# Constants of attention made in the projection, six query and key transfers a head, diagonal sums from a second column of ones

## The chip, the cores and the metric

The kernel runs on one core of a Trainium2 chip. The core has five engines with queues of their own: TensorE (PE; matmuls, results in PSUM), VectorE (DVE), ScalarE (ACT), GpSimd (POOL) and SyncE (SP, which here only issues transfers). They run freely and meet at semaphores. Sixteen DMA engines move data between HBM and SBUF. The metric is the device time of one execution in microseconds.

## The reference

The program computes four blocks with residuals on x of shape (2, 2048, 256). The change is in the first one, attention:

```python
x = x + attn_a(layernorm(x), Wq, Wk, Wv, Wc, terrace_mix, index_decays, mega_decays)
x = x + ffn(layernorm(x), ...)       # 16 experts, top 2, and a shared one
x = x + attn_b(layernorm(x), ...)    # gated linear attention over routed memories
x = x + ffn(layernorm(x), ...)

# attn_a: 16 heads of 16, segments of 64 rows
scores  = q @ k.T / 4, causal
out_t   = softmax(scores where the key's segment is the row's or the one before) @ v
att     = softmax(scores)
pcs     = (att * exp(index_decays)).sum(rows of a segment)          # (segments, L)
mega    = clip(exp(mega_decays * 64), 0, 2)
w       = scan over segments: carry = carry * mega + pcs, outputs the carry before
w       = w / (w.sum(-1) + 1e-5)
kv      = einsum(w, k, v);  out_lin = q @ kv
tw      = sigmoid(terrace_mix)
y       = (tw * out_t + (1 - tw) * out_lin) @ Wc.T
```

## The kernel before

The phases follow each other with a barrier of all engines between: `phase_project`, `phase_attend`, `phase_merge`, `phase_moe` (experts), `phase_route`, `phase_gla`, `phase_final`, `phase_moe`. A phase is one block with a hand-written order of instructions for each engine; semaphores named in the code tie them. There is no scheduler: what stands in a queue runs in that order.

`phase_project` (lines 78 to 338) takes x in eight stretches of 512 rows: layer norm, transposes, the products q, k and v. Queries and keys are split into three bf16 parts (`part`, SyncE stores them at line 135 to `q_parts` and `k_parts`, each [3, 512, 2048] in DRAM), since a float32 score is made of six bf16 products. Values are stored with a 17th column of ones per tile of 128 rows (`vv`, `EV = 17`, memset at line 156), so that a product with them yields the sum of the weights too. SyncE's last issues are `v_tok` and `k_tok` (lines 141 and 143), and it waits for them before the phase ends.

`phase_attend` (348 to 907) goes over 32 heads (2 batches of 16). A head has 16 tiles of 128 query rows; four tiles make a group (`QUADS`), so there are 128 groups, numbered g. Per group:
- TensorE writes a window of scores (`window`, line 745: for each tile its own 128 keys and the 64 before, with a mask) and then 4 or 6 blocks of up to 1024 scores of earlier keys (`scores`, 764). All go to a ring of three PSUM buffers `S`, so a block waits for the exponential three places before it (`s_E`).
- VectorE takes row minima (scores are negated) of the window (`window_minima`, 655) and of each block (`minima`, 663), ScalarE the exponentials (`window_exps` into `Tt`, 579, and `exps` into `E` with row sums into `rs`, 591).
- TensorE transposes the window's probabilities (`transposes`, 777), VectorE copies them out (`keep_transposed`, 683), TensorE multiplies them with the values (`values`, 797; `vs` holds the values shifted by 64 rows for the tiles' first halves), VectorE scales the result into `Y` (`outputs`, 689).
- The row sum of the window without the 64 keys that are also in a block, needed to join window and blocks, is a VectorE reduction of `Tt` (`diag_sums`, 670). GpSimd forms the weights of the parts (`differences` 510, `weights` 516), between its steps VectorE inverts the total (`inverses`, 679), and TensorE adds the weighted probabilities up into `pcs` (`sums`, 818), one group later, between the blocks of the next one.
- Once a head, GpSimd makes the outer products of keys and values (`products`, 537, in three portions of 5, 5 and 6), and TensorE, ScalarE and VectorE turn `pcs`, multiply and normalise (841 to 864, 604 to 620, 702).

A group's order on VectorE, from line 718: window minima of the next group, its blocks' minima with the copy of the transposed behind the second and inverses and outputs behind the third, then `tops`, `normalise` in the fourth group, `diag_sums`. SyncE loads queries, keys and values of a head one head ahead into two buffers (`load_qk`, `load_kv`). `sq` and `sk` hold six slots of 16 rows, pairs of parts.

The constants are made in `phase_attend`'s preface: five small loads on SyncE ahead of the first head (425 to 427), the gate `tw`, `eid` and sixteen `decay` blocks of 32x32 on ScalarE (570 to 576), a mask on GpSimd (507), three copies to the other partitions behind the loads of two heads (455), for which TensorE waits ahead of the second group: `pe.wait_ge(spread, 48)` (869).

In `phase_moe` GpSimd scatters rows to their experts (line 1288), 64 transfers one after another, and clears a buffer of blank rows ahead of them (1276 to 1278) in the first of the two calls.

## Time and profile before

| | us |
|---|---|
| median of 3 runs | 2676.49 |
| lowest and highest | 2672.58, 2676.88 |
| the profiled execution | 2675.66 |
| its span, first to last instruction | 2674.0 |
| projection | 0 to 127 |
| attention | 127 to 1252 |

A page gives busy times of each engine, waits by what released them, and groups of instructions by line. A timeline row has start, duration, engine, line, operation, names of what is written and read, shapes and count, and in brackets the engine's idle time before it with what ended it. Names have the phase's letters in front: `pj_` projection, `at_` attention, `am_` kept from attention to the merge, `m_` experts. PEld is the loading of a matmul's stationary operand. Stretches are given as start and end in us of the span.

### The profile page before, as it was taken

To read this page: it belongs to the slowest core of one execution; us is meant where nothing else is said; L and a number is where in the kernel's file an instruction comes from. 1 tells how busy PE (TensorE), PEld (TensorE's weight loads), DVE (VectorE), ACT (ScalarE), POOL (GpSimd) and SP (SyncE) were. 2 spreads that over 40 slices of the span, in tenths; PEclk is the share of its full clock that TensorE was granted. 3 is DMA by queue.
4 is the path that set the end of the run, shared out by engine and by line. 5 is a ranking of instruction groups with operands and counts; after the bars stand their busy time and mean duration, and the time that the engine had idled before them with its cause. 6 is when DMAs were issued, how large, how long until landed. Compare 5 with 4: busy or idle time off the path is not lost. (4 is left out here: it accounts for less than half of the span.)

```text
span 2674.0 us, 72919 instructions
## 1 busy us (share of the span) xinstructions
PE 2301.8 (86%) x27120; PEld 1535.0 (57%) x27120; DVE 1920.6 (72%) x4760; ACT 1564.0 (58%) x3827; POOL 1237.5 (46%) x2277
## 2 busy tenths in 40 slices
PE   8689999999999999997987944499999999688791
PEld 5435454454544544444756834377777777565681
DVE  6578888888888888884664656277777776476465
ACT  5467777777777777774352322366666665465230
POOL 3324444444444444445674536545544444247461
PEclk9879999999999999998898965699999999689896
DMA  6711111111112111112436644301111111553555
GB/s 217 244 47 38 39 38 39 39 36 38 35 37 65 36 37 38 39 38 83 147 121 205 219 163 170 108 21 50 50 46 50 50 40 32 173 190 122 144 156 200
DMA packets 187403, 243.45 MB, mean 91 GB/s; under 512 B 41400, under 2 KB 144709, under 8 KB 185136
## 3 DMA queue, kind: packets, MB, share of 16 engines
q1 hardware_dynamic: 160656, 182.07, 22.1%
q0 software_dynamic: 19872, 50.41, 5.5%
q10 hardware_dynamic: 6528, 6.31, 0.8%
q8 instruction: 222, 3.64, 0.6%
q14 instruction: 125, 1.02, 0.1%
HBM read 136.09 MB, written 106.50 MB: 91 GB/s over the span
## 5 line engine op out<-in xcount | busy, mean ns | idle before, releaser
L668 DVE TENSOR_REDUCE at_mn<-at_S 128x1 f32<-128x1024 f32 (+4 forms) x704 | 611.5, 880 | 113.5 <-PE at_S L773 107.9
L597 ACT ACTIVATE at_E<-at_S,at_mn 128x1024 f32<-128x1024 f32 (+4 forms) x704 | 596.0, 848 | 153.4 <-DVE at_mn L668 153.4
L813 PE MATMUL at_pcs<-at_E,at_c 128*32 128x256 f32 (+1 forms) x4864 | 432.7, 345 | 0.0
L773 PE MATMUL at_S<-at_sk,at_sq 96*128 96x512 bf16 (+3 forms) x1152 | 334.0, 354 | 37.0 <-ACT at_E L597 25.4
L546 POOL TENSOR_TENSOR at_kvo<-at_kh,at_vh 128x256 f32<-128x256 f32 x512 | 303.6, 627 | 0.0
L813 PEld LDWEIGHTS at_pcs<-at_E,at_c 128*32 128x32 f32 x4864 | 185.8, 108 | 86.5 <-issue 80.6
L587 ACT ACTIVATE at_Tt<-at_S,at_mn 128x192 f32<-128x192 f32 x512 | 173.2, 421 | 104.0 <-DVE at_mn L658 104.0
L1293 POOL DMA_INDIRECT expert_out<-m_ysb,m_dst x158 | 155.4, 984 | 131.5 <-DVE m_dst L1471 118.4
L813 PE MATMUL at_pcs<-at_Tt,at_c 128*32 128x128 f32 x1024 | 208.5, 286 | 0.0
L520 POOL TENSOR_TENSOR at_fr<-at_f,at_rs 128x12 f32<-128x12 f32 x128 | 27.2, 212 | 381.3 <-ACT at_f L602 381.3
L773 PEld LDWEIGHTS at_S<-at_sk,at_sq 96*128 96x128 bf16 x1152 | 78.6, 97 | 214.5 <-issue 91.9
L1601 PE MATMUL m_b<-m_wgu,m_xT 128*128 x632 | 167.4, 388 | 1.5 <-issue 1.0
L2535 PEld LDWEIGHTS gl_S<-gl_X,gl_Y 32*64 32x64 f32 (+1 forms) x8448 | 112.0, 129 | 64.0 <-issue 34.9
L2535 PE MATMUL gl_S<-gl_X,gl_Y 32*64 32x32 f32 (+2 forms) x8448 | 137.5, 226 | 12.4 <-ACT gl_A L2259 12.3
L597 ACT ACTIVATION_READ_ACCUMULATOR at_E<-at_S,at_mn 128x1 f32 x704 | 146.4, 208 | 0.0
L1346 ACT ACTIVATE m_sg<-m_b 128x128 f32<-128x128 f32 x158 | 43.8, 277 | 168.6 <-PE m_b L1601 168.6
L1601 PEld LDWEIGHTS m_b<-m_wgu,m_xT 128*128 128x128 f32 x632 | 120.7, 194 | 22.6 <-issue 6.2
L658 DVE TENSOR_REDUCE at_mn<-at_S 128x4 f32<-128x768 f32 x128 | 121.1, 946 | 12.1 <-PE at_S L759 12.1
L793 PEld LDWEIGHTS at_M<-at_ident,at_Tt 64*128 64x128 f32 x1024 | 83.1, 139 | 71.8 <-issue 65.0
L1476 DVE TENSOR_TENSOR m_hd<-m_sg,m_b 128x128 f32<-128x128 f32 x158 | 45.3, 287 | 109.5 <-ACT m_sg L1346 109.4
L793 PE MATMUL at_M<-at_ident,at_Tt 64*128 64x64 f32 x1024 | 117.4, 235 | 7.3 <-ACT at_pcsT L614 7.1
L2167 POOL DMA_INDIRECT expert_out<-gl_ysb,gl_dst x64 | 64.9, 1013 | 105.9 <-ACT gl_ysb L2283 93.7
(392 smaller groups left out, 5534.3 us busy)
## 6 DMA issues: line engine op xcount, KB each, us to landing
m_xg<-expert_rows SPq DMA_DIRECT2D x158, 129.0 KB
at_sq<-q_parts SPq DMA_DIRECT2D x192, 64.0 KB, 2.2
at_sk<-k_parts SPq DMA_DIRECT2D x192, 64.0 KB, 2.2
memory_rows<-m_blank SPq DMA_DIRECT2D x8, 1032.0 KB
gl_hx<-memory_rows SPq DMA_DIRECT2D x32, 258.0 KB, 3.8
m_wgu<-in_f_wgu SPq DMA_DIRECT2D x2, 4096.0 KB, 13.9
m_yin<-expert_out SPq DMA_DIRECT2D x8, 1024.0 KB, 6.9
rt_yin<-expert_out SPq DMA_DIRECT2D x7, 1024.0 KB, 10.2
```

Of the source, the lines that this page charges most:

```text
L546: ins = pool.tensor_tensor(kvo[:, t, 0:DH * DH].rearrange("p (d e) -> p d e", d=DH), k3[:, t, :].unsqueeze(2).to_broadcast([P, DH, DH]), v ...
L587: ins = nc.scalar.activation(Tt[:, q, s, :], S[v % NS_B][:, at:at + TW], ACT.Exp, bias=mn[:, q, s, 0:1], scale=-1.0)
L597: nc.scalar.activation(E[:, at:at + w], S[v % NS_B][:, 0:w], ACT.Exp, bias=mn[:, q, s, 1 + j:2 + j], scale=-1.0, accum_out=rs[:, q, s, 1 + ...
L658: nc.vector.tensor_reduce(mn[:, g % NQ, :, 0].rearrange("p (b s) -> p b s", b=2), S[v % NS_B][:, :].rearrange("p (b c) -> p b c", b=2)[:, ...
L668: nc.vector.tensor_reduce(mn[:, q, s, 1 + j:2 + j], S[v % NS_B][:, 0:w], AX.X, ALU.min).then_inc(s_mn, 1)
L773: ins = nc.tensor.matmul(S[v % NS_B][:, c:c + cw], sq[:, u, t * P:(t + 1) * P], sk[:, u, c0 + c:c0 + c + cw], start=True, stop=True)
L793: ins = nc.tensor.transpose(M[:, s * P + e * SEG:s * P + (e + 1) * SEG], Tt[half, q, s, e * SEG:e * SEG + P], ident[half, half])
L813: ins = nc.tensor.matmul(pcs[j * R:(j + 1) * R, cols[0]:cols[1]].rearrange("p (b c) -> p b c", c=P), lhsT, rhs, start=(n, j) not in touche ...
L1293: pool.indirect_dma_start(out=yb.rearrange("t (j d) -> (t j) d", j=TOPK), out_offset=bass.IndirectOffsetOnAxis(ap=dst[:, t, :], axis=0), i ...
L1601: ins = nc.tensor.matmul(bank[4 + t % 2][:, 0:2 * MH], xT[:, t % 2, k, :], wgu[:, k, ds(at, D)], start=(k == 0), stop=(k == KC - 1))
L2167: pool.indirect_dma_start(out=yb.rearrange("t (j d) -> (t j) d", j=TOPK), out_offset=bass.IndirectOffsetOnAxis(ap=dst[:, a, 2 * p + v, :], ...
L2535: return nc.tensor.matmul(out, Y[r_h, i % 2, l, u * P + keys:u * P + keys + out.shape[0]], queries, start=True, stop=True)
```

## The change

It does six things.

1. `EV` is 18: behind a tile's 16 value columns stand two of ones, and the second is zero in partitions 64 to 127. In `values` its product gives, for the first half of a tile's rows, the sum without the 64 keys before. `diag_sums` is gone; `outputs` copies the sums out of PSUM with two copies of 64 rows and 4 elements, and the weights wait for both (`s_ds`).
2. VectorE's `inverses` stands behind the fourth block's minima, `outputs` alone behind the third. On GpSimd a group's `products` go ahead of its `weights`.
3. The gate, `eid` and the decays are made in `phase_project`: the loads behind those of x, memset and iota with GpSimd's first work, the rest behind the last work of ScalarE, VectorE and GpSimd, the three copies behind SyncE's last store. The phase ends after they have landed. TensorE's wait in attention is gone.
4. `load_qk` sends three query and three key transfers instead of six and six.
5. x of the projection is loaded into the memory that attention's result has later (`stream`).
6. The clearing of the blank rows goes from GpSimd to VectorE, behind the last addition of the shared expert.

```diff
-EV = DH + 1
+EV = DH + 2
@@ phase_project, SyncE
+            for u in range(2):
+                sp.dma_start(tmix[u * SEG:(u + 1) * SEG, :], terrace_mix).then_inc(cin, 16)
+                sp.dma_start(dec[u * SEG:(u + 1) * SEG, :], index_decays).then_inc(cin, 16)
+            sp.dma_start(lam_raw[:, :], mega_decays.to_broadcast([R, H])).then_inc(cin, 16)
             for n in range(NS):
...
+            sp.wait_ge(cut, 1)
+            for j in range(1, P // R):
+                sp.dma_start(decay[j * R:(j + 1) * R, :, :], decay[0:R, :, :]).then_inc(spread, 16)
+            sp.wait_ge(spread, 16 * (P // R - 1))
             sp.wait_ge(tok_out, NS * 16)
@@ phase_project, GpSimd
+            pool.memset(v4[:, :, :, DH:EV], 1.0).then_inc(ones_set, 1)
+            pool.wait_ge(ones_set, 1)
+            pool.memset(v4[SEG:P, :, :, DH + 1:EV], 0.0).then_inc(ones_set, 1)
...
+            pool.wait_ge(g_p2, 2 * NS)
+            pool.wait_ge(cdone, 3 + H)
+            pool.affine_select(out=decay[0:R, :, :], in_=decay[0:R, :, :], compare_op=ALU.is_gt, fill=0.0, base=0,
+                               pattern=[[0, H], [1, R]], channel_multiplier=-1).then_inc(cut, 1)
@@ phase_project, ScalarE, behind its last work
+            nc.scalar.activation(tw[:, :], tmix[:, :], ACT.Sigmoid).then_inc(cdone, 1)
+            for u in range(2):
+                nc.scalar.activation(eid[u * SEG:(u + 1) * SEG, :, u], dec[u * SEG:(u + 1) * SEG, :],
+                                     ACT.Exp).then_inc(cdone, 1)
+            act.wait_ge(s_lam, 2)
+            for h in range(H):
+                nc.scalar.activation(decay[0:R, h, :], gap[:, :], ACT.Exp, scale=lam[:, h:h + 1]).then_inc(cdone, 1)
@@ phase_attend, SyncE
                 for lo, hi in Q_PARTS:
-                    for part in range(lo, hi):
-                        sp.dma_start(sq[slot * DH:(slot + 1) * DH, u, :],
-                                     q_parts[part, n * DH:(n + 1) * DH, :]).then_inc(qk_in[u], 16)
-                        slot += 1
+                    sp.dma_start(sq[slot * DH:(slot + hi - lo) * DH, u, :], q_parts[lo:hi, n * DH:(n + 1) * DH, :]
+                                 ).then_inc(qk_in[u], 16)
+                    slot += hi - lo
                 for part, reps in enumerate(K_REPS):
-                    for _ in range(reps):
-                        sp.dma_start(sk[slot * DH:(slot + 1) * DH, u, :],
-                                     k_parts[part, n * DH:(n + 1) * DH, :]).then_inc(qk_in[u], 16)
-                        slot += 1
+                    sp.dma_start(sk[slot * DH:(slot + reps) * DH, u, :],
+                                 k_parts[part:part + 1, n * DH:(n + 1) * DH, :].to_broadcast([reps, DH, L])
+                                 ).then_inc(qk_in[u], 16)
+                    slot += reps
@@ phase_attend, GpSimd
-                pool.wait_ge(s_ds, g + 1)
+                pool.wait_ge(s_ds, 2 * g + 2)
...
-                weights(g)
                 if q == 3:
                     products(n, 0, 5)
...
+                weights(g)
@@ phase_attend, VectorE
-            def diag_sums(g):
-                dve.wait_ge(s_E, unit(g, 0) + 1)
-                nc.vector.tensor_reduce(rs[:, g % NQ, :, 0], Tt[:, g % NQ, :, SEG:TW], AX.X, ALU.add).then_inc(s_ds, 1)
...
                 dve.wait_ge(s_O, g + 1)
+                nc.vector.tensor_copy(rs[0:SEG, q, :, 0], o[0:SEG, :, DH + 1]).then_inc(s_ds, 1)
+                nc.vector.tensor_copy(rs[SEG:P, q, :, 0], o[SEG:P, :, DH]).then_inc(s_ds, 1)
...
                     if k == 3:
+                        outputs(g)
+                    if k == 4:
                         inverses(g)
-                        outputs(g)
@@ phase_attend, TensorE
-            pe.wait_ge(spread, 48)
@@ phase_moe, from GpSimd to VectorE
+                nc.vector.memset(blank[:, :, 0:D], 0.0).then_inc(blanked, 1)
```

SyncE at the start of attention, before. `at_tmix`, `at_dec` and `at_lam_raw` are the constants, `at_kh`, `at_vh` and `at_vs` keys and values of a head by rows:

```order
L425 DMA at_tmix<-in_a_mix 64x1
L426 DMA at_dec<-in_a_index_decays 64x16
L425 DMA at_tmix<-in_a_mix 64x1
L426 DMA at_dec<-in_a_index_decays 64x16
L427 DMA at_lam_raw<-in_a_mega_decays 32x16
L433 DMA at_sq<-q_parts 16x2048 x6
L439 DMA at_sk<-k_parts 16x2048 x6
L445 DMA at_kh<-k_tok 128x256
```

The same place now, with the end of the projection ahead of it:

```order
L152 DMA k_tok<-pj_kk 128x16x128
L156 DMA am_decay<-am_decay 32x512 x3
L81 UNCONDITIONAL_BRANCH
L453 UNCONDITIONAL_BRANCH
L458 DMA at_sq<-q_parts 48x1x2048
L458 DMA at_sq<-q_parts 32x1x2048
L458 DMA at_sq<-q_parts 16x2048
L463 DMA at_sk<-k_parts 48x1x2048
L463 DMA at_sk<-k_parts 32x1x2048
L463 DMA at_sk<-k_parts 16x2048
L470 DMA at_kh<-k_tok 128x256
```

The constants have left the place ahead of the first queries, the copies of the decays stand in the phase before, and twelve transfers of 16 rows have become six of 48, 32 and 16.

VectorE over one group of attention, before, from the window minima on:

```order
L658 TENSOR_REDUCE at_mn<-at_S 128x4
L668 TENSOR_REDUCE at_mn<-at_S 128x1 x2
L687 COPY at_TTs<-at_M 128x512
L668 TENSOR_REDUCE at_mn<-at_S 128x1
L681 RECIPROCAL at_inv<-at_tot 128x4
L694 RECIPROCAL at_inv_t<-at_M 128x4
L697 SCALAR_TENSOR_TENSOR stream<-at_M,at_tw,at_inv_t 128x2x16 x2
L668 TENSOR_REDUCE at_mn<-at_S 128x1 x3
L677 TENSOR_REDUCE at_top<-at_mn 128x4
L672 TENSOR_REDUCE at_rs<-at_Tt 128x4
```

The same group now:

```order
L658 TENSOR_REDUCE at_mn<-at_S 128x4
L668 TENSOR_REDUCE at_mn<-at_S 128x1 x2
L683 COPY at_TTs<-at_M 128x512
L668 TENSOR_REDUCE at_mn<-at_S 128x1
L690 COPY at_rs<-at_M 64x4
L691 COPY at_rs<-at_M 64x4
L692 RECIPROCAL at_inv_t<-at_M 128x4
L695 SCALAR_TENSOR_TENSOR stream<-at_M,am_gate,at_inv_t 128x2x16 x2
L668 TENSOR_REDUCE at_mn<-at_S 128x1
L677 RECIPROCAL at_inv<-at_tot 128x4
L668 TENSOR_REDUCE at_mn<-at_S 128x1 x2
```

The reduction at the group's end is gone, two copies stand behind the third block, and the inverse has moved from ahead of the outputs to behind the fourth block.

## Rows read from the trace of the kernel before

**Rows 1.** The page: span, and busy time of each engine.
```profile
span 2674.0 us, 72919 instructions
PE 2301.8 (86%) x27120; PEld 1535.0 (57%) x27120; DVE 1920.6 (72%) x4760; ACT 1564.0 (58%) x3827; POOL 1237.5 (46%) x2277
```

**Rows 2.** Windows: stretch, length, busy by engine, then PEclk, DMA share, GB/s.
```profile
134.00:137.00 3.00, 0.00 (x0) 0.00 (x0) 0.00 (x0) 3.00 (x15) 0.00 (x0) 0.50 0.43 131
168.00:170.00 2.00, 2.00 (x14) 0.55 (x13) 1.25 (x2) 0.00 (x0) 0.00 (x0) 0.69 0.00 0
300.00:600.00 300.00, 287.16 (x3357) 149.67 (x3357) 266.09 (x506) 231.14 (x591) 125.55 (x355) 1.00 0.14 37
```

**Rows 3.** Timeline, end of projection and first group: start, us, engine, what, idle before.
```profile
116.37 3.42 SPq L143 DMA_DIRECT2D k_tok<-pj_kk  x1
...
127.00 0.58 SPq L425 DMA_DIRECT2D at_tmix<-in_a_mix  x1
...
130.15 3.00 SPq L433 DMA_DIRECT2D at_sq<-q_parts  x6
...
133.20 2.73 SPq L439 DMA_DIRECT2D at_sk<-k_parts  x6
...
133.85 3.50 ACT L576 ACTIVATE at_decay<-at_gap,at_lam 32x32 f32<-32x32 f32 x16
...
137.76 0.48 PE L753 MATMUL at_S<-at_mask,at_identb 128*128 128x384 bf16 x1 [23.84 <-DMA at_sk<-k_parts]
...
143.55 0.23 ACT L597 ACTIVATION_READ_ACCUMULATOR at_E<-at_S,at_mn 128x1 f32 x1
...
149.26 0.50 PE L753 MATMUL at_S<-at_mask,at_identb 128*128 128x384 bf16 x1 [5.59 <-DMA at_decay<-at_decay]
```

**Rows 4.** Waits of SyncE, 0 to 150 us: for whom, us in total, times, longest.
```profile
SPq L80 <- DMA k_tok<-pj_kk: 6.1, 1, 6.1
```

**Rows 5.** The page's DMA issues: count, KB each, median us to landing.
```profile
at_sq<-q_parts SPq DMA_DIRECT2D x192, 64.0 KB, 2.2
```

**Rows 6.** Groups by line and form: count, busy us, mean ns, idle before.
```profile
L672 DVE TENSOR_REDUCE at_rs<-at_Tt 128x4 f32<-128x512 f32 x128 | 86.3, 675 | 0.0
...
L1405 DVE COPY ready_rows<-m_idx_f 128x4 f32<-128x4 f32 x8 | 1.5, 190 | 0.0
```

**Rows 7.** Timeline in the steady stretch: VectorE, then GpSimd, ScalarE, TensorE.
```profile
504.08 1.23 DVE L668 TENSOR_REDUCE at_mn<-at_S 128x1 f32<-128x1024 f32 x1 [0.29 <-PE at_S L773]
505.22 0.17 DVE L681 RECIPROCAL at_inv<-at_tot 128x4 f32<-128x4 f32 x1
505.31 0.15 DVE L694 RECIPROCAL at_inv_t<-at_M 128x4 f32<-128x4 f32 x1
...
505.82 1.59 DVE L668 TENSOR_REDUCE at_mn<-at_S 128x1 f32<-128x256 f32 x2
...
504.02 0.21 POOL L520 TENSOR_TENSOR at_fr<-at_f,at_rs 128x12 f32<-128x12 f32 x1 [3.22 <-ACT at_f L602]
...
504.58 0.20 POOL L524 TENSOR_TENSOR at_tot<-at_tot,at_fr 128x4 f32<-128x4 f32 x1
...
507.44 1.11 ACT L597 ACTIVATE at_E<-at_S,at_mn 128x1024 f32<-128x1024 f32 x1 [0.44 <-DVE at_mn L668]
...
509.26 0.43 PE L793 MATMUL at_M<-at_ident,at_Tt 64*128 64x64 f32 x4 [0.23 <-ACT at_pcsT L614]
...
522.54 0.23 PE L805 MATMUL at_M<-at_vs,at_TTs 128*64 128x17 f32 x1 [0.18 <-DVE at_TTs L687]
...
529.11 0.61 PE L773 MATMUL at_S<-at_sk,at_sq 96*128 96x512 bf16 x2 [0.21 <-ACT at_Tt L587]
```

**Rows 8.** Blank rows: one VectorE line's durations (min/median/max ns), then timeline rows.
```profile
L1386 DVE TENSOR_SCALAR m_ex<-m_ex x16: 195/196/856, 1323.0 to 2456.7; 128x64 f32<-128x64 f32 x16
...
1328.99 1.22 POOL L1288 DMA_INDIRECT expert_rows<-m_rows,m_slot  x1 [5.23 <-DVE m_slot L1429]
...
1418.68 0.22 DVE L1471 SCALAR_TENSOR_TENSOR m_dst<-m_xg,m_e_tab 128x1 uint32<-128x1 f32 x1 [18.24 <-DMA m_xg<-expert_rows]
```

More of the change, by code:

```diff
@@ L103, in phase_project @@
         p_k = [m.ps(f"k{j}", [P, 2, D]) for j in range(2)]
+        tmix, dec = m.sb("tmix", [P, 1]), m.sb("dec", [P, H])
+        lam, lam_raw = m.sb("lam", [R, H]), m.sb("lam_raw", [R, H])
+        gap, gap_i = m.sb("gap", [R, R]), m.sb("gap_i", [R, R], mybir.dt.int32)
+        cin, cmade, s_lam, cdone, cut, spread = (m.sem(k) for k in ("const_in", "const_made", "lam", "const_done", "cut", "spread"))
         w_in, made, ones_set = m.sem("w_in"), m.sem("made"), m.sem("ones_set")
@@ L423, in _ @@
         def _(sp):
-            for u in range(2):
-                sp.dma_start(tmix[u * SEG:(u + 1) * SEG, :], terrace_mix).then_inc(cin, 16)
-                sp.dma_start(dec[u * SEG:(u + 1) * SEG, :], index_decays).then_inc(cin, 16)
-            sp.dma_start(lam_raw[:, :], mega_decays.to_broadcast([R, H])).then_inc(cin, 16)
             def load_qk(n):
@@ L452, in _ @@
                 load_kv(n)
-            sp.wait_ge(made, 11)
-            for j in range(1, P // R):
-                sp.dma_start(decay[j * R:(j + 1) * R, :, :], decay[0:R, :, :]).then_inc(spread, 16)
             for n in range(NHEAD):
@@ L487, in _ @@
             pool.wait_ge(made, 5)
-            pool.memset(eid[:, :, :], 0.0).then_inc(made, 1)
-            pool.wait_ge(made, 6)
-            pool.iota(gap_i[:, :], pattern=[[1, R]], base=-1, channel_multiplier=-1).then_inc(made, 1)
-            pool.wait_ge(made, 7)
             pool.tensor_copy(identb[:, :], ident[:, :]).then_inc(made, 1)
@@ L505, in _ @@
             pool.wait_ge(s_ready, 2)
-            pool.wait_ge(cdone, 3 + H)
-            pool.affine_select(out=decay[0:R, :, :], in_=decay[0:R, :, :], compare_op=ALU.is_gt, fill=0.0, base=0,
-                               pattern=[[0, H], [1, R]], channel_multiplier=-1).then_inc(made, 1)
             def differences(g):
@@ L567, in _ @@
         def _(act):
-            act.wait_ge(cin, 80)
-            act.wait_ge(made, 7)
-            nc.scalar.activation(tw[:, :], tmix[:, :], ACT.Sigmoid).then_inc(cdone, 1)
-            for u in range(2):
-                nc.scalar.activation(eid[u * SEG:(u + 1) * SEG, :, u], dec[u * SEG:(u + 1) * SEG, :],
-                                     ACT.Exp).then_inc(cdone, 1)
-            act.wait_ge(s_lam, 2)
-            for h in range(H):
-                nc.scalar.activation(decay[0:R, h, :], gap[:, :], ACT.Exp, scale=lam[:, h:h + 1]).then_inc(cdone, 1)
             act.wait_ge(s_ready, 2)
@@ L742, in _ @@
         def _(pe):
-            pe.wait_ge(made, 10)
+            pe.wait_ge(made, 8)
             def window(g):
@@ L1274, in _ @@
                 scale_of(k)
-            if x_out is None:
-                pool.memset(blank[:, :, 0:D], 0.0).then_inc(blanked, 1)
-                pool.memset(blank[:, :, D:D + 1], FAR).then_inc(blanked, 1)
-                pool.memset(blank[:, :, D + 1:XW], 0.0).then_inc(blanked, 2)
             for n in range(NS):
@@ L1466, in _ @@
             add_shared(NS - 1)
+            if x_out is None:
+                nc.vector.memset(blank[:, :, 0:D], 0.0).then_inc(blanked, 1)
+                nc.vector.memset(blank[:, :, D:D + 1], FAR).then_inc(blanked, 1)
+                nc.vector.memset(blank[:, :, D + 1:XW], 0.0).then_inc(blanked, 2)
             for t in range(NTILE + 2):
```

53 lines of the change are left out of this document (27 added, 26 removed).

## The prediction

> **What bounds the kernel now.** I read the page first. Its chain of waits covers a few per cent and ends in the second expert layer, so it says nothing of attention; TensorE is busy for 86% of a span of 2674.0 us [rows 1]. Next come the windows. In attention's steady stretch, 300 to 600 us, TensorE is busy for 287.16 us of 300 at full granted clock, VectorE for 266.09, ScalarE for 231.14, GpSimd for 125.55 [rows 2]. So TensorE bounds attention. VectorE is close behind it, and an edit there counts only where TensorE waits for what VectorE releases. Then the timeline at the seam of projection and attention, the one place where every compute engine stands still: the last key-row store is issued at 116.37, SyncE waits 6.1 us for it to land, attention's first transfer is issued at 127.00, TensorE starts at 137.76 after 23.84 us, and stands again for 5.59 us until 149.26, waiting for the copied decays [rows 3, 4].
>
> **Preface of attention, what goes.** Before, SyncE issues five loads of constants from 127.00 (some 0.62 us each), then twelve loads of query and key parts from 130.15 (3.00 us for six, 2.73 for the next six), and TensorE starts 2.3 us after the last issue began at about 135.5 [rows 3]. Now six transfers stand first. Their bytes are the same, 12 x 64 KB a head.
>
> What they take is not in the trace, since every row of it has 16 rows or a multiple outermost on both sides. I bound it from both sides by those rows. From 134 to 137 us only such loads move: 131 GB/s at a share of 0.43 of 16 engines, or 19.0 GB/s for one engine [rows 2]. **Wide case**: a transfer is spread over 16 engines as before. 0.79 MB at 304 GB/s is 2.6 us and hidden behind the issues: the sixth starts at 127.0 + 5 x 0.5 = 129.5, TensorE starts at 131.8, that is 6.0 us earlier. **Narrow case**: four of the six now have 3 or 2 as outermost size of their source pattern (three parts, two parts, or a key part repeated three or two times), and a transfer that is dealt out by its outermost rows goes to 3 or 2 engines. Then the first two engines carry 64 KB of each of these four and 4 KB of each of the two others, 264 KB or 0.270 MB, which at 19.0 GB/s is 14.2 us. A 64 KB load lands 2.2 us after issue [rows 5], of which 0.2 is its 4 KB per engine, so 2.0 us are fixed, and TensorE starts at 127.0 + 2.0 + 14.2 = 143.2, which is 5.4 us later than now. I take the narrow case: equal shares of three outer rows can't be cut for 16 engines, and nothing in the trace shows an outer size under 16 spread wide. If one engine alone is faster than its share among sixteen, the loss shrinks; at double the rate it is 127.0 + 2.0 + 7.1 = 136.1, a gain of 1.7. I keep all three for the range.
>
> The Trainium skill has a rule that speaks against this edit. By "DMA: Bandwidth & Descriptors", section "Why a DMA increments its semaphore by 16 and not by 1", a transfer runs on the largest number of engines up to 16 that divides the slowest dimension of both patterns, and its guidance table says that a leading zero-stride broadcast of c copies confines it to at most c. No row here shows it. The same page states some 27 GiB/s for an engine; with that figure an estimate gives 264 KB in 9.3 us and a start at 138.3, 0.6 later than now.
>
> In later heads the loads are sent a head ahead: 14.2 us of queue against a head of about 33 us (300 us of the windows hold nine heads of four groups) stays hidden, at nothing. Value rows for a head queue behind them and are needed 25 us after they are sent.
>
> **The wait for decays** goes: they are ready before attention starts. Without it TensorE is next stopped by the third exponential of the first group, whose last piece ends at 143.78 [rows 3], so the second group starts at about 143.8, not 149.26: 5.4 us gained. In the narrow case all of the preface is 5.4 later, so the first group ends at 149.1 and the second starts where it does now: +5.4 - 5.4 = 0. In the wide case the two gains add: -11.4.
>
> **What the constants cost at projection's end.** ScalarE has 6.8 us of them (two table loads 1.28 each, 16 decays 3.50, the rest 1), free from 114.7, so to 121.5; GpSimd's mask less than 1 us more, to some 122.4; three copies on SyncE's queue behind the key rows [rows 3]. These rows land until about 125.9, 6.1 us after SyncE's last issue ended at 119.79 [rows 3, 4]. 192 KB more at 304 GB/s is 0.65 us, the wider value rows (64 KB) 0.2. I take +0.9, from +0.2 (copies slip between) to +1.6. The loads of the constants stand behind x on SyncE, idle until 25.7 us; the memsets more on GpSimd there are over long before ScalarE's first value copy.
>
> **Clock.** TensorE's granted clock is 0.50 in the preface (1.2 GHz), 0.69 in the mean of 168 to 170 us and 1.00 (2.4 GHz) in the steady stretch [rows 2], so it rises at about 169. Before that TensorE paused for 5.59 us until 149.26 [rows 3]. Without the pause the rise may come up to about as much sooner, and time at half the clock is worth half: 0 to -3; I take -1.
>
> **Steady state, per head.** VectorE loses one reduction of 0.68 us a group [rows 6], at the group's end, and gains two copies of 64x4 out of PSUM in the chain behind a group's third block. Their nearest rows are 0.15 us for a reciprocal of 128x4 out of PSUM [rows 7] and 0.19 for a copy of 128x4 [rows 6]; back to back such operations start 0.09 us apart (505.22 to 505.31) [rows 7]. I take 0.09 each, up to 0.2. What counts is the edges to TensorE:
> - Gain: window minima start up to 0.6 earlier. TensorE waits on that chain only twice a head, 0.21 us at 529.11 (window exponentials) and 0.18 at 522.54 (copy of transposed probabilities) [rows 7]. Both close: -0.39.
> - Loss one: the sum of the diagonal now comes after the values, so GpSimd's weights start later, and the inverse (now behind the fourth block) waits for them in VectorE's queue; behind it are the fifth block's minima, its exponential and TensorE's next scores. From the end T of the third block's minima: copies end T + 0.15, GpSimd starts at + 0.08 and takes 0.77 (504.02 to 504.78) [rows 7], the inverse starts at T + 1.03, the fifth block at T + 1.12. Now it starts at T + 0.87 (506.18, the row of 505.82 less its second minimum of 1.23, against T = 505.31), so +0.25, and it reaches TensorE whole, which already waits there (ScalarE for VectorE 0.44 at 507.44, TensorE 0.23 at 509.26) [rows 7]. That is in the third group of a head; in the second and fourth the block's scores come later anyway, and it costs nothing.
> - Loss two: where the next group has four blocks, the inverse stands behind an 896-wide minimum and the weights reach TensorE at T + 2.4, about 0.1 after it wants them, where they now have 1.5 us to spare: +0.1.
>
> GpSimd's products, now ahead of the weights, end at 503.8 in the group shown, before the weights can start: nothing. A value matmul of 18 columns for 17: eight pairs start 0.06 apart, one seventeenth more of it is at most 3.5 us in all, I take +1. Sum: (-0.39 + 0.25 + 0.1) = -0.04 a head, -1 for 31 heads, +1 for columns: **0**. If each small operation takes 0.1 more, this is +0.2 to +0.6 a head, up to +19; if the fifth block never waits, -0.29 a head, -9.
>
> **The rest.** At the tail five of the sixteen last products go ahead of the last weights instead of behind; GpSimd has the same work either way: nothing. The blank rows' memset leaves GpSimd, where it ran beside a VectorE operation that took 856 ns there and 196 in the median of its 16 times, on the way to the first slots, for which GpSimd waited 5.23 us; its scatters then follow each other to the end of the stage, so that 0.66 goes through [rows 8]. On VectorE it lands in an idle stretch of 18.24 us [rows 8].
>
> **Sum, narrow case**: +5.4 - 5.4 + 0.9 - 1 + 0 - 0.66 = -0.8. The profiled execution took 2675.66, so 2674.9; the runs' median is 0.83 above it, so **2675.7**. A measurement tells about 0.2%, 5.4 us, from no change.
>
> **Rivals.** (a) Wide transfers: -11.4 + 0.9 - 1 + 0 - 0.66 = -12.2, so 2664.3. For it: equal bytes, and the engines of all loads of before are equally used. Against it: the outer sizes. (b) VectorE gains a real share: each head also wins what VectorE has less to do, the low end of the steady sum: -9 and -2 more of clock, 2665 even with narrow transfers. Against it: TensorE's idle time is 12.8 of 300 us, and what is not named above follows its own scores through VectorE and ScalarE. (c) Slower: the inverse's wait in VectorE's queue. It costs 0.25 a head as sized; it decides from the point where the round over GpSimd takes 1.4 us from T, not 1.03, because then the second and fourth group pay as well, +0.6 a head or +19 us: 2695 narrow. (d) The change does what it says but one engine is faster than its share: -3 to -7 on the forecast.
>
> **How the numbers follow.** Forecast 0.47 (2669 to 2683 of its own), wide 0.24, VectorE's gain and faster single engines 0.15, slower 0.14. Faster by over 5.4 us holds the wide case and most of the third: 0.37. Same: 0.48. Slower: the fourth and the forecast's upper end: 0.15. The range leaves out half of the fourth and the far end of the wide case: 2661 to 2684.
>
> **What would show it.** Landing times of the six transfers (2.2 us wide, 10 and more narrow) and TensorE's first start against 131.8, 136.1 or 143.2 on the old scale; the second group at 143.8 or 149.2; the end of projection 0.9 later; VectorE's inverse with idle time before it that names GpSimd, 0.2 to 0.5 us in three groups of four; TensorE's waits of 0.21 and 0.18 gone and its idle share in a steady stretch unchanged at 4%; the time of 36 groups in 300 us. The forecast is wrong if the transfers spread wide, or if a head gets shorter by over 0.15 us.

## The result and the profile after

The changed kernel takes 2699.65 us in the median of 4 runs (2697.09 to 2703.5), against 2676.68 of the kernel before: a ratio of 1.0091 (95% interval 1.0073 to 1.0108), **23 us slower**. The forecast was 2675.7 with a range from 2661 to 2684. The profiled execution took 2697.09.

Its page, in the place of [rows 1]:

```profile
span 2695.4 us, 72858 instructions
PE 2315.9 (86%) x27120; PEld 1537.3 (57%) x27120; DVE 1887.5 (70%) x4891; ACT 1569.7 (58%) x3827; POOL 1235.0 (46%) x2275
```

VectorE has 33 us less to do than before, as meant, and the kernel is longer. TensorE is busy for 14 us more although its products are the same in number; part of that is time at half its clock, below.

**The preface came as forecast.** The timeline of the changed kernel, SyncE and TensorE (start, us, engine, what; compare [rows 3]):

```profile
122.53 3.18 SPq L156 DMA_DIRECT2D am_decay<-am_decay  x3
128.25 2.04 SPq L458 DMA_DIRECT2D at_sq<-q_parts  x3
130.34 1.97 SPq L463 DMA_DIRECT2D at_sk<-k_parts  x3
...
142.99 0.48 PE L750 MATMUL at_S<-at_mask,at_identb 128*128 128x384 bf16 x1 [28.85 <-DMA at_sk<-k_parts]
...
149.03 0.50 PE L750 MATMUL at_S<-at_mask,at_identb 128*128 128x384 bf16 x1 [0.17 <-ACT at_E L603]
```

TensorE starts at 142.99 (forecast for the narrow case 143.2, in the kernel before 137.76), waits for the transfers for 28.85 us, and the second group starts at 149.03 (forecast 149.2, before 149.26). The wait for the decays is gone and the later start has eaten it. The windows at that place show how few engines carry the loads (stretch, length, busy by engine, clock, DMA share, GB/s):

```profile
133.00:136.00 3.00, 0.00 (x0) 0.00 (x0) 0.00 (x0) 0.00 (x0) 0.00 (x0) 0.50 0.71 192
136.00:139.00 3.00, 0.00 (x0) 0.00 (x0) 0.00 (x0) 0.00 (x0) 0.00 (x0) 0.50 0.20 72
```

From 133 to 136 us the value and key rows of `load_kv`, which are spread wide, run beside them; behind these a share of 0.20 of 16 engines is left, that is 3.2 engines, while TensorE still waits.

**The steady heads did not.** I take the first mask product of a head as its start. The rows of the changed kernel at two successive heads, and TensorE's waits between them:

```profile
487.60 0.33 PE L750 MATMUL at_S<-at_mask,at_identb 128*128 128x384 bf16 x1
...
521.95 0.33 PE L750 MATMUL at_S<-at_mask,at_identb 128*128 128x384 bf16 x1
...
530.70 0.30 PE L810 MATMUL at_pcs<-at_Tt,at_c 128*32 128x128 f32 x1 [0.22 <-POOL at_c L547]
...
539.41 0.28 PE L770 MATMUL at_S<-at_sk,at_sq 96*128 96x256 bf16 x1 [0.87 <-ACT at_E L603]
...
547.79 0.34 PE L770 MATMUL at_S<-at_sk,at_sq 96*128 96x384 bf16 x1 [0.53 <-ACT at_E L603]
```

and of the kernel before, at the same place:

```profile
483.25 0.33 PE L753 MATMUL at_S<-at_mask,at_identb 128*128 128x384 bf16 x1
...
517.21 0.33 PE L753 MATMUL at_S<-at_mask,at_identb 128*128 128x384 bf16 x1
```

A head takes 34.35 us, before 33.96. The waits of 0.21 and 0.18 [rows 7] are gone as forecast; in their place stand 0.22 for GpSimd's weights and 0.53 for an exponential, and a wait that took 0.77 (at 500.71) takes 0.87. Split into four stretches, each from the first mask product of a group to that of the next, a head was 7.82, 7.71, 8.63 and 9.80 us and is 7.71, 7.72, 8.71 and 10.20. TensorE meets a delay of VectorE's chain early in the stretch after the one in which it arises: the 0.53 in the fourth stretch comes from the blocks of the third group, which is what the forecast's "third group" means. TensorE's busy time in the steady stretch, 287.16 of 300 before [rows 2]:

```profile
300.00:600.00 300.00, 284.27 (x3309) 147.69 (x3304) 253.12 (x533) 230.25 (x585) 123.34 (x349) 1.00 0.12 37
```

**And TensorE's clock falls in mid-attention**, which it never does between heads 1 and 31 of the kernel before. Four heads (numbers 14, 20, 25 and 31 of 0 to 31) have a third stretch of 11.72 to 11.76 us; in the first three of them the fourth is 0.8 shorter, so a fall costs 2.2 us net. The timeline at the first of them:

```profile
642.45 0.28 PE L770 MATMUL at_S<-at_sk,at_sq 96*128 96x256 bf16 x1 [0.87 <-ACT at_E L603]
```

and the windows around it:

```profile
641.00:645.00 4.00, 3.13 (x35) 1.85 (x34) 3.27 (x7) 3.81 (x12) 2.71 (x6) 0.94 0.15 59
645.00:649.00 4.00, 4.00 (x35) 1.73 (x29) 2.62 (x8) 1.80 (x4) 1.38 (x4) 0.50 0.42 123
649.00:651.00 2.00, 2.00 (x15) 0.33 (x10) 0.91 (x3) 0.84 (x4) 0.63 (x3) 0.50 0.14 35
651.00:655.00 4.00, 4.00 (x41) 2.28 (x35) 3.11 (x6) 3.11 (x8) 0.21 (x1) 0.96 0.00 0
```

After TensorE's wait of 0.87 us the granted clock goes from 1.00 to 0.50 (1.2 GHz) at about 644.5 and comes back after 651. The same wait stands in every head, and only four of them have a fall.

**The account.** Head 31 starts at 1196.44 before and at 1215.47 now, 19.0 later: 0.1 from all of the preface and head 0, 1.1 in head 1, 29 x 0.39 = 11.3 in heads 2 to 30, 6.6 in three falls. Head 31 adds 2.8 up to its fourth group (3.0 of its fall, less 0.2 in its second stretch), so there it is 21.8. The merge's first product comes 19.6 later (1276.0 against 1256.4), so 2.2 come back in the tail. The traces show where: the kernel before has a fall of its own there, with a clock of 0.51 from 1241 to 1248 us, and the changed kernel has 1.00 at the same work, from 1263 to 1269. One row of TensorE from the tail, before and now:

```profile
1243.56 3.65 PE L856 MATMUL at_M<-at_kvo,at_pcsT 128*32 128x257 f32 x32 [3.78 <-issue]
```

```profile
1264.25 1.94 PE L853 MATMUL at_M<-at_kvo,at_pcsT 128*32 128x257 f32 x32 [2.65 <-issue]
```

At the end of the span the difference is 21.4; I have nothing on the 1.8 behind the merge's start.

### The profile page after: what moved, and what is told of

Its sections match the earlier page's. It is cut to its first block and busy times, and to the rows that moved or that the text cites. A ratio compares the mean times of both kernels' runs of the same rounds, so it can differ in the third digit from the quotient of the medians.

```text
span 2695.4 us, 72858 instructions
## 1 busy us (share of the span) xinstructions
PE 2315.9 (86%) x27120; PEld 1537.3 (57%) x27120; DVE 1887.5 (70%) x4891; ACT 1569.7 (58%) x3827; POOL 1235.0 (46%) x2275
## 5 line engine op out<-in xcount | busy, mean ns | idle before, releaser
L810 PE MATMUL at_pcs<-at_E,at_c 128*32 128x256 f32 (+1 forms) x4864 | 439.2, 350 | 0.0
L527 POOL TENSOR_TENSOR at_diff<-at_mn,at_top 128x12 f32<-128x12 f32 x128 | 26.7, 209 | 217.1 <-DVE at_top L673 217.1
```

The source lines that it names most:

```text
L810: ins = nc.tensor.matmul(pcs[j * R:(j + 1) * R, cols[0]:cols[1]].rearrange("p (b c) -> p b c", c=P), lhsT, rhs, start=(n, j) not in touche ...
```

## Experiments

Times below are compared with the kernel before, run beside them. Beside the first four kernels it took 2770.89 us. A steady head with the sums of before has the same length there to 0.02 us, so the difference lies outside of the heads, and those four are judged by ratio and by their rows in attention. For a kernel that ran only once, steps under 5 us are read from its trace alone.

### Which part costs

**Sums as before in the changed kernel**, the rest of the change kept:

```diff
-EV = DH + 2
+EV = DH + 1
-                nc.vector.tensor_copy(rs[0:SEG, q, :, 0], o[0:SEG, :, DH + 1]).then_inc(s_ds, 1)
-                nc.vector.tensor_copy(rs[SEG:P, q, :, 0], o[SEG:P, :, DH]).then_inc(s_ds, 1)
+                nc.vector.tensor_reduce(rs[:, g % NQ, :, 0], Tt[:, g % NQ, :, SEG:TW], AX.X, ALU.add).then_inc(s_ds, 1)
...
```

> The changed kernel with the tile sums as before: one column of ones, the VectorE reduction of each group, the inverse before the outputs, GpSimd's products behind the weights. Everything else is the change (constants in the projection, six transfers, blank rows on VectorE). Theory (the sums cost 0.39 us a head, and the four falls of the granted clock in the middle of attention come from their longer waits): heads of 33.96 us, no fall of the clock after 169 us, 2699.65 - 12 - 9.7 = 2678. Rival (the falls come from something else that the change brings): heads of 33.96 us with falls of the clock still, 2688. Rival two (heads are longer for another reason): 34.35 us a head and about 2699.

Measured: ratio 0.998 (0.9964 to 0.9995), 2763.4 against 2770.89; heads of 33.97 us, no fall of the clock, TensorE's start at 142.72 and head 31's at 1196.92, 0.5 later than before. So constants, narrow transfers and the blank rows together are worth little up to the end of attention, as the forecast's sum said. The ratio stands for 5 us less all the same; they arise behind head 31's start, and no run takes them apart.

**The new sums alone in the kernel before**, the same edit the other way round:

> The kernel before with nothing but the tile sums changed: two columns of ones, two 64x4 copies out of PSUM in place of the reduction, inverse behind the fourth block, products ahead of the weights. Theory: heads of 34.35 us instead of 33.96 and some falls of TensorE's clock, 2676.7 + 12 + 10 = about 2698. Without falls of the clock 2688.5; if the sums are not the cause, 2677.

Measured: ratio 1.0084 (1.0051 to 1.0117), heads of 34.35 us, four falls (heads 15, 20, 25, 30). The loss is the sums', nearly whole, and so are the falls: they come with the sums and go with them.

### The transfers

**Sixteen outer rows.** Only the order of rows within `sq` and `sk` changes, in both alike, so the products are the same:

```diff
-q_parts[lo:hi, n * DH:(n + 1) * DH, :]
+q_parts[lo:hi, n * DH:(n + 1) * DH, :].rearrange("p d l -> d p l")
...
-k_parts[part:part + 1, n * DH:(n + 1) * DH, :].to_broadcast([reps, DH, L])
+k_parts[part, n * DH:(n + 1) * DH, :].unsqueeze(1).to_broadcast([DH, reps, L])
```

> The changed kernel with the same six transfers a head, but every pattern has 16 rows outermost on both sides (row d of all parts, then row d + 1), so that bytes and the number of transfers stay and only the outermost size goes from 3 or 2 to 16. Theory (a transfer with 3 or 2 outer rows is confined to few engines): the sixth load is issued at about 131.6 us and lands 2.2 us later, TensorE starts attention at about 133.8 instead of 142.99, the second group starts at about 139.9 instead of 149.03, and the median falls by 9 us, from 2699.65 to about 2690.5. Rival (what takes long is a transfer of 48 or 32 rows, however it is cut): start at 143 and 2699.6 as now. The steady heads stay at 34.35 us under both.

Its SyncE rows and TensorE's first product, and then its window from 130 to 133 us:

```profile
127.03 1.85 SPq L458 DMA_DIRECT2D at_sq<-q_parts  x3
128.92 1.80 SPq L464 DMA_DIRECT2D at_sk<-k_parts  x3
...
133.36 0.48 PE L751 MATMUL at_S<-at_mask,at_identb 128*128 128x384 bf16 x1 [20.43 <-DMA at_sk<-k_parts]
```

```profile
130.00:133.00 3.00, 0.00 (x0) 0.00 (x0) 0.00 (x0) 0.00 (x0) 1.64 (x6) 0.50 0.82 222
```

From the first issue to TensorE's start it is 6.3 us instead of 14.7, with a DMA share of 0.82 while they run; head 31 starts 10.5 us sooner than in the changed kernel (1204.94 against 1215.47, three falls instead of four). Ratio to the kernel before 1.0034 (1.002 to 1.0047): the sums' loss is still in it. The narrow case is shown: outermost size 3 or 2 against 16, with the same bytes and the same number of transfers. By the Trainium skill's rule ("DMA: Bandwidth & Descriptors", section "Why a DMA increments its semaphore by 16 and not by 1") these transfers go to 3, 2 and 16 engines, and the trace agrees (3.2 engines' share, and 8.4 us regained).

**Both together**, wide transfers and sums as before, twice:

> Both of the above: constants in the projection, six transfers with 16 outer rows, sums as before. Theory: TensorE starts at about 133.8 and the second group at 139.9, heads of 33.96 us, no fall of the clock: 2678 - 9 = 2669, 7 to 8 us faster than the kernel before. If the transfers' outer size does nothing it is 2678.

> Six wide transfers, constants in the projection and sums as before once more, beside the one-column version on one chip: TensorE starts at 133.9, heads of 33.96 us, 8.4 us under the kernel before (ratio 0.997), 7 over the one-column version.

Measured: 0.9961 (0.9937 to 0.9985) and, the second time, 2665.98 against 2676.92, 0.9961 (0.9947 to 0.9975). TensorE starts at 133.89 and 134.44, heads of 33.96 to 33.97, no fall, head 31 at 1188.03 and 1186.18. That is what the change brings without the sums and with transfers that use all engines: 11 us.

**Twelve loads of 16 rows** in the same kernel (`load_qk` as before the change):

> Constants in the projection, sums as before, but twelve loads of 16 rows. Theory (issues of 0.5 us bound the start when transfers are wide): first issue 128.25, the twelfth begins at about 133.8, TensorE starts at 136.1, 2.2 us later than with six wide transfers and 6.6 sooner than with six narrow ones; second group at 142.2: ratio 0.9975. Rival (the number of loads does nothing): 133.9.

Measured: 2667.74, 0.9964 (0.995 to 0.9978), TensorE's start at 134.37. From the first issue (126.74) that is 7.63 us, against 6.33 to 6.56 with six wide ones. I had expected the start 1.7 later, since SyncE reached it earlier here; the number of loads is worth 1.2 us. This kernel is 9.2 us under the one before, and its head 31 starts 7.5 sooner (1188.93 against 1196.44), so most of the 11 comes from moving the constants out of the preface, with its wait for the decays; the blank rows moved to VectorE are in this kernel too and have no run of their own.

### What in the sums costs

Rows of VectorE in the changed kernel, behind the third block of a third group (compare the first rows of [rows 7], the same place; "third group" by its blocks):

```profile
508.43 1.22 DVE L668 TENSOR_REDUCE at_mn<-at_S 128x1 f32<-128x1024 f32 x1 [0.28 <-PE at_S L770]
509.57 0.14 DVE L690 COPY at_rs<-at_M 64x4 f32<-64x4 f32 x1
509.74 0.17 DVE L691 COPY at_rs<-at_M 64x4 f32<-64x4 f32 x1
509.94 0.18 DVE L692 RECIPROCAL at_inv_t<-at_M 128x4 f32<-128x4 f32 x1
510.16 0.41 DVE L695 SCALAR_TENSOR_TENSOR stream<-at_M,am_gate,at_inv_t 128x32 f32<-128x32 f32 x2
510.49 0.41 DVE L668 TENSOR_REDUCE at_mn<-at_S 128x1 f32<-128x256 f32 x1
510.86 0.18 DVE L677 RECIPROCAL at_inv<-at_tot 128x4 f32<-128x4 f32 x1
510.95 1.93 DVE L668 TENSOR_REDUCE at_mn<-at_S 128x1 f32<-128x1024 f32 x2
```

From the first copy to the reciprocal it is 0.37 us (509.57 to 509.94), where I had put 2 x 0.09; from the first copy to the fifth block 1.38 (510.95), where from the same point it was 0.96 (505.22 to 506.18). Four kernels take it apart. The first has one copy:

```diff
-                nc.vector.tensor_copy(rs[0:SEG, q, :, 0], o[0:SEG, :, DH + 1]).then_inc(s_ds, 1)
-                nc.vector.tensor_copy(rs[SEG:P, q, :, 0], o[SEG:P, :, DH]).then_inc(s_ds, 1)
+                nc.vector.tensor_copy(rs[:, q, :, 0], o[:, :, DH]).then_inc(s_ds, 2)
```

> The changed kernel with one copy of 128x4 out of PSUM in place of the two of 64x4 (column of the whole window for all rows, so the first half of each tile gets a sum that holds the preceding rows too: a part of the computation is changed). Read by the length of a steady head and the falls of the granted clock. Theory (what lengthens a head is the start of the fifth block's minima, 0.41 us later, of which the two copies are 0.38): a copy's pitch of 0.18 less, so TensorE's waits of 0.53 and 0.87 a head fall to 0.35 and 0.77 and the one for GpSimd's weights from 0.22 to 0.04: head 34.35 - 0.18 - 0.10 - 0.18 = 33.9. Rival (the place of the inverse and of GpSimd's products does it, not the copies): 34.3. If the falls of the clock come from TensorE's added waits, there are none or one here.

Measured: a head of 33.73 us (7.57, 7.54, 8.61, 10.01), no fall, 2669.58 in one run against 2677.21. Faster than expected, and its rows say why:

```profile
513.06 1.22 DVE L668 TENSOR_REDUCE at_mn<-at_S 128x1 f32<-128x1024 f32 x1 [0.41 <-PE at_S L769]
514.20 0.15 DVE L690 COPY at_rs<-at_M 128x4 f32<-128x4 f32 x1
514.27 0.17 DVE L691 RECIPROCAL at_inv_t<-at_M 128x4 f32<-128x4 f32 x1
```

The full-height copy takes 0.07 us of the queue, not half of 0.37.

**No copy** (both lines out, GpSimd waits for `s_O`, `rs` set to 1 at the start):

> The changed kernel without the two copies (the weights use a constant 1 in place of the diagonal's sum, so this part of the computation is left out; GpSimd waits for the values in their place). Theory: the fifth block starts 0.38 earlier, head 34.35 - 0.38 - 0.10 - 0.22 = 33.65, 0.3 under the kernel before, which is what the sums could have brought had the copies cost nothing. Rival (order): 34.2 or more. No fall of the clock if the added waits cause it.

Measured: a head of 33.47 us (7.58, 7.47, 8.61, 9.81), no fall, 2656.79 in one run. TensorE's waits from 300 to 600 us, changed kernel first, then this one (line waited for: us in total, times, longest):

```profile
PE at_S L770 <- ACT at_E L603: 11.7, 17, 0.9
PE at_M L790 <- ACT at_pcsT L620: 2.1, 9, 0.2
PE at_pcs L810 <- POOL at_c L547: 1.9, 9, 0.2
```

```profile
PE at_S L768 <- ACT at_E L603: 6.9, 9, 0.8
PE at_M L788 <- ACT at_pcsT L620: 2.1, 9, 0.2
```

So taking the reduction away, in the new order, was worth 0.49 us a head (33.96 to 33.47), and the two half-height copies cost 0.88 (to 34.35). The rival, that the new order costs, is out: with it and without the copies a head is shorter than before.

**The copies twice** (the same two lines again into a tile `again` that nobody reads):

> The changed kernel with the two copies made a second time into memory that nobody reads, so twice the cost. Theory: the fifth block starts 0.37 later once more, and TensorE, which already waits for it in two groups of a head, waits that much more in both: head 34.35 + 0.74 = 35.1, and at least as many falls of the clock as 4. Rival (copies are hidden): 34.35.

Measured: a head of 35.14 us (8.04, 7.98, 8.77, 10.34), six falls, 2737.53 in one run. That the length agrees with the sum is luck: of the 0.79 more, 0.33 and 0.26 lie in the first and second stretch and 0.06 and 0.14 in the third and fourth, the two I had put 0.37 on each, and TensorE has a new wait of up to 0.3 for VectorE's outputs (2.6 us in 8 times, from 200 to 500 us). Its four half-height copies and the reciprocal start at 305.65, 305.83, 306.03, 306.19 and 306.37: 0.16 to 0.20 apart.

**The inverse directly behind the outputs:**

```diff
                     if k == 3:
                         outputs(g)
-                    if k == 4:
                         inverses(g)
```

> The changed kernel with the inverse directly behind the outputs, ahead of the fourth block's minima. In the changed kernel the total is ready 0.25 us behind the outputs' end (545.17 against 544.92). Theory: the inverse waits about 0.29 us in VectorE's queue with the fourth and the fifth block behind it, the weights come some 0.4 sooner: +0.29 in two groups of a head, -0.22: head 34.7. Rival (its place behind the fourth block is what costs): head 34.1.

Measured: a head of 35.15 us (7.71, 8.35, 8.81, 10.28), four falls, 2729.8 in one run. In VectorE's rows the inverse waits 0.29 us for GpSimd's total in each group, as sized; the head lost 0.80, where I had 0.35. Of that, 0.63 is in the second stretch, where TensorE has a wait that the changed kernel hasn't, for VectorE's `normalise` once a head:

```profile
585.16 0.43 PE L789 MATMUL at_M<-at_ident,at_Tt 64*128 64x64 f32 x4 [0.51 <-DVE at_kvn L709]
```

So its place behind the fourth block, which the change chose, is right for these sums, and my sum missed an edge to TensorE altogether.

**Half height or number?** Two, and then seven, copies of full height:

> The changed kernel with two copies of full height (128x4) in place of the two of half height; the second goes to memory that nobody reads, and the first gives the first half of each tile the whole window's sum (a part of the computation is changed). Theory (half height costs, number does not): the copies start 0.08 us apart, the reciprocal 0.15 behind the first, a head 33.73 + 0.3 = 34.0 at most, no fall of the clock. Rival (each further copy costs 0.18): 34.35 as in the changed kernel, with falls.

> The same with seven copies of full height, six of them unread. Theory: 6 x 0.08 = 0.48 more in VectorE's chain than with one, 0.18 more than the two half-height copies cost, so a head of 34.35 + 0.4 = 34.75 us; and falls of TensorE's clock in mid-attention as in the changed kernel (4 or more), since its waits are at least as long. Rival (the falls go with the half-height copies): the same head without a fall.

Measured: a head of 33.80 us with two and no fall; 34.39 with seven and three falls (one run each, 2668.4 and 2700.72, beside 2675.86). Rows of the kernel with seven, where the copies start 0.07 apart:

```profile
507.61 0.15 DVE L691 COPY at_rs<-at_M 128x4 f32<-128x4 f32 x1
507.68 0.15 DVE L692 COPY at_again<-at_M 128x4 f32<-128x4 f32 x1
507.75 0.15 DVE L693 COPY at_again<-at_M 128x4 f32<-128x4 f32 x1
...
508.02 0.15 DVE L697 COPY at_again<-at_M 128x4 f32<-128x4 f32 x1
508.09 0.17 DVE L698 RECIPROCAL at_inv_t<-at_M 128x4 f32<-128x4 f32 x1
```

Seven full copies (0.48 us) cost a head about what the two half-height ones (0.37) did. I had expected 34.75 with seven; the head is less sensitive there than my sum made it.

What makes the half-height copies dear is that they start at different rows (0 and 64), not that they are short. In the changed kernel's rows each of them and the reciprocal behind starts 0.03 us after the end of the one ahead (509.57 + 0.14, then 509.74; 509.74 + 0.17, then 509.94), while full-height ones start 0.08 before that end. Operations on 32 rows that start at row 0, like their neighbours, do that too, in the same kernel:

```profile
530.01 0.17 DVE L673 TENSOR_REDUCE at_top<-at_mn 128x4 f32<-128x12 f32 x1
530.10 0.14 DVE L703 TENSOR_SCALAR at_den<-at_M 32x1 f32<-32x1 f32 x1
...
530.45 0.47 DVE L709 TENSOR_SCALAR at_kvn<-at_M,at_rden 32x256 f32<-32x256 f32 x1
530.85 0.94 DVE L658 TENSOR_REDUCE at_mn<-at_S 128x4 f32<-128x768 f32 x1
```

The one of 32 rows at 530.10 starts 0.08 before the reduction ahead ends, and the one of 128 rows at 530.85 starts 0.07 before the one of 32 rows ends.

### The falls of the clock

Sixteen traces, sorted by the length of a steady head, with the number of falls in heads 1 to 31:

| head, us | kernels | falls |
|---|---|---|
| 33.47 to 33.80 | no copy, one-column early (below), one copy, one-column (below), two full copies | 0 in each |
| 33.96 to 33.97 | before, sums as before, wide with sums as before (twice), twelve loads | 0 in each |
| 34.35 to 34.37 | changed, new sums alone, wide | 4, 4, 3 |
| 34.39 | seven full copies | 3 |
| 35.14, 35.15 | copies twice, inverse at 3 | 6, 4 |

The falls come where TensorE waits more, whatever makes it wait: seven full-height copies bring them without any half-height one. From 300 to 600 us its named waits are 11.8 us in the kernel before and 12.2 in the one-column version, without falls, and 15.7 in the changed kernel. This is a correlation over sixteen traces. Where in the heads they come differs from kernel to kernel, and nothing here shows how the chip decides it.

### A version that beats both

One copy is enough with the right result too, if the second column of ones is left all ones in memory and zeroed in SBUF for the preceding rows only, after each load, by GpSimd, a head ahead:

```diff
+            def clear_preceding(n):
+                pool.wait_ge(kv_in[n % 2], (n // 2 + 1) * KV_LOADS)
+                pool.memset(vs[0:SEG, n % 2, :].rearrange("p (t e) -> p t e", e=EV)[:, :, DH + 1:EV], 0.0
+                            ).then_inc(s_cl, 1)
...
+                nc.vector.tensor_copy(rs[:, q, :, 0], o[:, :, DH + 1]).then_inc(s_ds, 2)
...
+                    pe.wait_ge(s_cl, n + 1)
```

> A version meant to beat both: the changed kernel with 16 outer rows for the six transfers and ONE copy of 128x4 a group with the reference's result: the second column of ones is all ones in memory, and GpSimd zeroes it for the preceding rows after each head's load (a memset of 64x16 a head, behind the load and ahead of the head's first values). Theory (the number of copies in front of the fourth block's minima sets the head): head 33.7 as with one copy, against 33.96 of the kernel before, TensorE starts at 133.4 instead of 137.76, no fall of the clock in mid-attention: 8.4 + 30 x 0.23 = 15 us under the kernel before, ratio 0.994. Rival (the memset on GpSimd, or TensorE's wait for it, takes the gain): head 33.96, ratio 0.997.

Measured: 2657.26 against 2676.92, 0.9934 (0.9917 to 0.9951); heads of 33.73 us, no fall. The memset takes 0.12 us a head. VectorE's inverse does wait 0.2 us for GpSimd's total in this version, once a head. Then the weights in another order, with what does not need the diagonal ahead of the wait for it:

```diff
-                pool.wait_ge(s_ds, 2 * g + 2)
-                pool.tensor_tensor(fr[:, :, :], f[:, q, :, :], rs[:, q, :, :], ALU.mult)...
+                pool.tensor_tensor(fr[:, :, 1:KK], f[:, q, :, 1:KK], rs[:, q, :, 1:KK], ALU.mult)...
+                pool.tensor_tensor(tot2[:, :], fr[:, :, 1], fr[:, :, 2], ALU.add)...
+                pool.wait_ge(s_ds, 2 * g + 2)
+                pool.tensor_tensor(fr[:, :, 0], f[:, q, :, 0], rs[:, q, :, 0], ALU.mult)...
```

> As the one-column version, with GpSimd's product and sum over the two exponential columns made ahead of its wait for the diagonal, so that one operation less (0.27 us) stands between the copy and the inverse. Theory: the inverse, which stands behind the fourth block's minima, does not wait now, so only TensorE's wait for weights can shrink, which is already near 0: the same as the one-column version within 0.1 us a head. Rival (the round over GpSimd still bounds a group): 0.2 a head less, 6 us.

Measured: **2653.51, ratio 0.9909 (0.9893 to 0.9926)**, 23 us under the kernel before and, by the medians, 46 under the changed one. A head takes 33.57 us; the fourth group went from 10.01 to 9.83, since the inverse no longer waits for GpSimd there (one such wait from 300 to 600 us instead of nine). I had expected nothing from this; the rival was right in kind (0.16 of its 0.2 a head). The intervals of the two versions overlap, so the 3.7 us between their medians rest on the head's length in the traces.

## Why the prediction was wrong

- **Transfers, first start, second group:** right, on the narrow case. 142.99 and 149.03 against 143.2 and 149.2. Their own time was a bit shorter than sized: 14.7 us from the first issue instead of 16.2, so some 12.7 for 0.270 MB behind the 2.0 that are fixed, or 21 GB/s for the engine against the 19.0 taken. The other estimate, a start at 138.3, was 4.7 us too early. SyncE started 1.25 later than before, in the range 0.2 to 1.6.
- **Wait for decays:** right, +5.4 - 5.4 = 0; and with wide transfers the second group comes at 139.41, 9.8 us earlier than before, most of the 11.4 that the wide rival named.
- **Clock in the preface, -1:** not seen. Head 1 starts at 177.91 against 177.78. The third group of head 0, in which the clock rises, takes 12.4 before and 12.8 now, and 10.2 to 12.8 in the others with no order that I can see.
- **The step that failed: two copies at 0.09 each.** I took the pitch of reciprocals that cover all 128 rows (505.22 to 505.31 in [rows 7]) for copies that cover 64, and named 0.2 as the end of the range without asking which of the two a half-height operation is nearer to. The two were put at 0.18 together and take 0.37, 0.17 from the first to the second and 0.20 from there to the reciprocal; one full copy takes 0.07. The sensitivity was in the prediction (+0.2 to +0.6 a head if each small operation takes 0.1 more, and +0.39 was measured), but the range from 2661 to 2684 left it out.
- **In how many groups a delay on VectorE counts.** The sum charged +0.25 for the third group and +0.1 elsewhere. The two copies cost 0.13, 0.25, 0.10 and 0.39 in the four stretches (changed kernel less the one with no copy), 0.88 together; the 0.39 is the third group's. There the path was as told, fifth block 0.4 later and a wait of 0.53 where none was, but the copies alone make that delay: the inverse, which the forecast had waiting for GpSimd, starts at 510.86 without idle time. In the second and fourth group I had put nothing, since their scores come later anyway. VectorE waited there for TensorE by 0.2 to 0.4 us, and a delay of 0.37 uses that up.
- **The gain:** 0.39 forecast, 0.49 there with no copy. A new wait of 0.22 for GpSimd's weights then stood in its place (loss two, put at 0.1).
- **Rival (c)** had the right sign and nearly the right size (+0.6 a head; measured +0.39) but another place: no inverse waits in VectorE's queue in the changed kernel, and where it was made to, it cost 0.80 more. It was given 0.14.
- **The falls of the clock,** 6.6 us up to head 31 and 3 more in it, stood in no term and no rival. I had a clock term for the preface only, since the steady stretch had 1.00 throughout [rows 2], and so put the clock there at nothing. The trace of before has a fall at the end of attention (0.51 from 1241 to 1248 us), which I did not read; when one would come in mid-attention it does not say.
- **Blank rows:** the VectorE line of 856 ns has 195 ns in the median and 250 at most now. The merge's first product comes 19.6 us after its old time, the first scatter 17.0, the first product of the sorted rows with the experts' weights 18.4. So 2.6 are won and 1.4 lost again on the way; how much of it is the blank rows' no run shows, and 0.66 decides nothing.

By the steps: 0 from the preface, 12.4 from heads 1 to 30, 9.6 from four falls, -2.2 in the tail, against -0.8 forecast for all of it.

## What to carry to other kernels

An operation that replaces a longer one is to be priced by what it does to its queue, and at the place where it stands: 0.68 us off a place with slack against 0.37 in the chain that every group waits for was a loss of 0.39 a head. Let small VectorE operations that follow each other start at the same row, at full height rather than in two halves, even at the cost of a memset elsewhere. When several parts are to be read from memory by one transfer, order the pattern so that its outermost size is 16 or a multiple of it on both sides, a repeated part included: here it cost nothing and head 31 started 8 to 10 us sooner.

## What the runs showed of the hardware

- VectorE operations on 128x4 that follow each other start 0.07 us apart (seven in a row), those on rows 0 to 63 and 64 to 127 in turn 0.16 to 0.20 apart (four in a row), though each takes 0.14 to 0.18 either way. The Trainium skill ("VectorE: DVE Perf Modes", section "Two Vector instructions with no wait between them") says, as a model, that an instruction whose operand starts in another group of 32 rows than the last one's is held until all earlier ones have finished. The rows agree: second copy and reciprocal start in another group than the instruction ahead, and it is these that are late, while operations of 32 rows that start at row 0 like their neighbours are not.
- Transfers of 192 and 128 KB with outermost size 3 or 2 left 3.2 of 16 engines' share busy and ran at some 21 GB/s for the engine that carries most (an estimate from 0.270 MB in 12.7 us); with outermost size 16 the same six took 6.3 us from first issue to use instead of 14.7. A 192 KB transfer spread wide landed 3.4 us after its issue in the median and one of 64 KB among them 3.1, where one of 64 KB took 2.2 in the kernel before.
- TensorE's granted clock can fall to 0.50 in the middle of steady work: in the changed kernel four times for some 7 us, 2.2 us of time each for the first three; with seven full copies three times for some 10 us, 4.7 us each (heads of 39.08 against 34.39). Between heads 1 and 31 of the kernel before it never did. A small wait more a head cost almost as much again in this way (9.6 us) as by itself (12.4).
